# Last layer of a four-layer kernel: new due times for a batch's turned rows and folded keys

## What is computed

```python
var = jnp.mean(jnp.square(hidden_states), axis=-1, keepdims=True)
normed = hidden_states * jax.lax.rsqrt(var + EPS) * norm_w
q = split_heads(normed @ wq)              # 16 heads of 64
k = split_heads(key_value_states @ wk)    # 77 keys per batch
v = split_heads(key_value_states @ wv)
attn = softmax(einsum('bhqd,bhkd->bhqk', q, k))
ctx = einsum('bhqk,bhkd->bhqd', attn, v)
return hidden_states + ctx @ wo
```

## Time and profile before

| | |
|---|---|
| median of 3 runs | 2225.31 us (2221.91 to 2230.49) |
| time of the profiled execution | 2232.05 us |
| its span (first to last instruction) | 2230.3 us |
| mean granted clock of TensorE | 0.971 of 2.4 GHz |
| last layer in the profile | 1875.7 to 2230.3 us |
| borders in the last layer | about 1950, 2036 and 2122 us |

### The profile page before, as it was taken

The page is one execution under the profiler, slowest core; times in us unless marked ns, Lnnn a source line. Parts: engine busy times, 40 slices in busy tenths (PEclk is TensorE's granted clock), DMA queues, the critical chain, the costliest instruction groups (busy, mean ns, idle before and its releaser), DMA issues. The chain is left out here.

```text
span 2230.3 us, 38605 instructions
## 1 busy us (share of the span) xinstructions
PE 2013.3 (90%) x14610; PEld 1309.0 (59%) x14610; DVE 1386.9 (62%) x3054; ACT 1137.6 (51%) x1750; POOL 769.4 (34%) x1012
## 2 busy tenths in 40 slices
PE   4999999999998879998999899998989998999989
PEld 2333433343342258876566575765666667888989
DVE  4876776685767655645545554451677884866655
ACT  2265565555545666651645545363445553555444
POOL 3023124113212353311624526253111201756656
PEclk8799999999998999998999999999999999999999
DMA  6705403510730000018460716320422210000000
GB/s 146 140 7 113 60 1 68 89 23 36 113 76 1 1 15 1 1 55 122 92 108 21 143 17 131 66 66 1 162 86 86 85 58 1 11 10 13 16 13 20
DMA packets 77774, 126.68 MB, mean 57 GB/s; under 512 B 16650, under 2 KB 34826, under 8 KB 77582
## 3 DMA queue, kind: packets, MB, share of 16 engines
q1 hardware_dynamic: 74966, 122.63, 26.0%
q10 hardware_dynamic: 2624, 1.58, 0.2%
HBM read 93.59 MB, written 30.32 MB: 56 GB/s over the span
## 5 line engine op out<-in xcount | busy, mean ns | idle before, releaser
L1099 DVE TENSOR_REDUCE nmx_causal<-banks 128x1 f32<-128x333 f32 (+4 forms) x896 | 435.6, 538 | 174.1 <-PE banks L830 172.3
L988 ACT ACTIVATE probs_causal<-banks 128x1024 f32<-128x1024 f32 (+5 forms) x384 | 330.8, 899 | 258.3 <-PE banks L855 254.4
L830 PE MATMUL banks<-ks_causal,qs_causal 96*128 96x333 bf16 (+4 forms) x896 | 271.7, 339 | 13.8 <-DVE nmx_causal L1099 7.6
L753 POOL TENSOR_SCALAR_AFFINE_SELECT probs_window<-probs_window 128x512 f32<-128x512 f32 (+1 forms) x272 | 162.0, 602 | 258.0 <-ACT probs_window L988 247.0
L753 POOL TENSOR_SCALAR_AFFINE_SELECT probs_causal<-probs_causal 128x512 f32<-128x512 f32 (+2 forms) x160 | 92.4, 578 | 455.7 <-ACT probs_causal L988 455.4
L855 PE MATMUL banks<-qs_causal,ks_causal 97*128 97x512 bf16 (+5 forms) x896 | 209.6, 329 | 19.8 <-ACT probs_causal L988 16.0
L1099 DVE TENSOR_REDUCE nmx_window<-banks 128x2 f32<-128x384 f32 (+2 forms) x320 | 143.0, 460 | 104.5 <-PE banks L830 100.8
L879 PE MATMUL banks<-probs_causal,v_causal 128*17 128x512 f32 (+5 forms) x1792 | 185.8, 488 | 0.0
L988 ACT ACTIVATE probs_window<-banks 128x768 f32<-128x768 f32 (+2 forms) x128 | 99.7, 785 | 102.6 <-PE banks L855 102.1
L828 PEld LDWEIGHTS banks<-below,identb 128*128 128x128 bf16 x512 | 49.4, 98 | 173.5 <-DVE nmx_causal L1099 125.2
L830 PEld LDWEIGHTS banks<-ks_causal,qs_causal 96*128 96x128 bf16 x896 | 86.5, 99 | 103.5 <-DVE nmx_causal L1099 60.9
(11 more groups left out here) (261 smaller groups left out, 4099.9 us busy)
## 6 DMA issues: line engine op xcount, KB each, us to landing
fs_masked<-in_fside SPq DMA_DIRECT2D x32, 616.0 KB, 3.7
ks_causal<-zk SPq DMA_DIRECT2D x96, 137.6 KB
ks_window<-zk SPq DMA_DIRECT2D x96, 137.6 KB
qs_causal<-zq SPq DMA_DIRECT2D x96, 128.0 KB
qs_window<-zq SPq DMA_DIRECT2D x96, 128.0 KB
zk<-parts_causal SPq DMA_DIRECT2D x24, 275.2 KB, 2.9
zk<-parts_window SPq DMA_DIRECT2D x24, 275.2 KB, 2.4
zq<-parts_causal SPq DMA_DIRECT2D x24, 256.0 KB, 6.9
```

What stands on the lines that cost most here:

```text
L753: pool.affine_select(out=v, in_=v, compare_op=ALU.is_ge, fill=0.0, base=const, pattern=[[0, QH], [by_c, wd]], channel_multiplier=by_p).the ...
L830: ins = pe.matmul(bk[:, c:c + m], qs[q][0:KR, h, t * P:(t + 1) * P], ks[q][0:KR, h, key:key + m], start=cover is None, stop=True, skip_gro ...
L988: ins = act.activation(dst, src, ACT.Exp, scale=DH ** -0.5)
L1099: dve.tensor_reduce(dst, src, AX.X, ALU.max, negate=True).then_inc(emptied_v, 1)
```

## The change

Three due times of `folded_schedule` are changed. No instruction is added, removed or resized, and no semaphore or tile.

```diff
@@ folded_schedule @@
         if b:
             early = t0 - 8
             for half in range(2):
                 for k in range(ND):
-                    fill(t0 - 1.65 + (2 * half + k) / 10, ("turn", b, half, k), "sv")
+                    fill(t0 - 7.4 + 9 * half + k, ("turn", b, half, k), "sv")
         else:
             early = t0 - 4
             for half in range(2):
                 for k in range(ND):
-                    fill(early + (2 * half + k) / 10, ("turn", b, half, k), "sv")
+                    fill(early + 6 * half + k / 10, ("turn", b, half, k), "sv")
         pool += [(early, ("kbd", b)), (t0 + 0.2, ("vbd", b, 0)), (t0 + 0.2, ("vbd", b, 1))]
         for n, (pp, kk) in enumerate((pp, kk) for pp in range(4) for kk in range(ND)):
-            fill((t0 - 1.6 if b else t0 - 3) + n / 8, ("fold", b, kk, pp), "sv")
+            fill(t0 - 2.7 + n / 4 if b else t0 - 3 + n / 8, ("fold", b, kk, pp), "sv")
```

## The result

The changed kernel takes 2238.28 us (median of 12 runs, 2232.28 to 2248.55), the kernel before 2226.52 us (12 runs, 2220.52 to 2236.55). The ratio is 1.0054, 95% interval 1.0037 to 1.0071: slower by 0.54%, some 12 us (8 to 16).

The account below looks back on a forecast made before the run. PE was taken to bind except at borders and the layer's start, where the loop around two banks binds. Borders of +3.6, +1.75 and +1.75 us and -1.5 at the start gave +5.6: 2231 us, range 2216 to 2240.

Parts of the forecast that it names:

- A: First half's turns moved early, before the border: transposes wait for DVE to empty a bank; +3.45 us, +3.85 at batch 1.
- C: Second half's turns moved late, behind the border: transposes wait for DVE; +2.5 us, +3.4 at batch 1.
- B: Border stretch, tile 7's score to next batch's second score: shorter mostly because turns left; -4.2 us, -3.7 at batch 1.
- D: Start of the last layer: two turns leave the head, first score 1.8 us earlier, some lost on DVE; -1.5 us.
- signs of being wrong: No long waits at line 2286, border stretch above 20 us, or clock below 0.9 in the windows behind A.
- clock rival: Clock falls to 1.2 GHz behind A, 2.3 us each, three times: +12.5 us, 2238 us; chance 0.10.
- B brings nothing: At borders, DVE's shift and invert within the folds cost as much as the turns did: 2243 us; chance 0.09.
- A and C hidden: Transposes behind the moved turns need not wait, 0.8 us each: -8.8 us, 2216.5 us; chance 0.15.
- the whole border saved: All waits at the three borders go, 7.6 us each: 25.2 us faster, 2200 us; chance 0.08.

Follow-up runs that it names:

- run 1: Kernel before with only the first half's two turns per batch moved early, ahead of the border; ratio to the kernel before 1.0025, 2242.34 us beside 2233.99.
- run 2: Kernel before with only the second half's two turns per batch moved late, behind the border; ratio to the kernel before 0.9995.
- run 5: Changed kernel with each batch's four turns each directly behind a tile's last transposes, in front of 21 matmuls; ratio to the kernel before 0.9965.
- run 6: Changed kernel with 24 unread identity transposes filling PE's wait behind the first half's second turn; ratio to the kernel before 1.0040.
- run 7: run 5's kernel with the eight folds of a batch spread over the border; ratio to the kernel before 0.9876, 2202.20 us.
- run 3: Kernel before with only the folds' due times changed; ratio to the kernel before 0.9993.
- run 4: Kernel before with only the layer's start changed, two turns of batch 0 behind scores 0 1 0; one profiled execution, 2238.78 us.
- run 8: run 7's kernel with out part 0 of tile 5 in front of tile 6's transposes, except in the last batch; ratio to the kernel before 0.9883, 2204.65 us.

## Why the prediction was right in kind and too small

It said +5.6 us and no measurable change, 2216 to 2240; it came out at +12 us (8 to 16), inside the range, at its slow end. By its own line of 0.5% the measured 0.54% is just on the slower side, to which it gave 0.21; the interval, 0.37 to 0.71, lies on both sides of that line.

**A** held to 0.03 us where the clock was full: 3.42 at batch 3 for 3.45, 3.85 at batch 1 for 3.85. **C** held: 2.57 for 2.5, 3.50 for 3.4. That a transposition two places behind a turn waits for DVE's shift and invert is shown by putting the wait in by itself (runs 1 and 2) and by taking it away: in run 5 the waits at line 2286 for a turn are gone, and A at batch 3 takes 3.05 us less, at full clock in both traces.

**B** was forecast at -4.2 and read -3.4 at batches 2 and 3; run 5 has -4.3 at full clock. So there the walk was right and the clock took 0.8 to 0.9. At batch 1 the forecast was -3.7 and -2.6 was read, at a clock of 0.83 (1958.18:1977.72 above). There the walk had a term that was too large: it put 1.0 us for norm36 and close36 among the folds (and its 18.4 is 18.26 by its own terms), but at a like clock batch 1's B is longer than batch 3's by only 0.15 us in run 5 and 0.5 in run 6, and in run 7, at full clock, all three are equal. So the clock took more than 1.1 at that border, and the two misses partly cancelled. Its reading, that the leaving turns and not the folds' pace shorten the border, is shown by runs 1 to 3.

**D** was -1.87 for -1.5. The first score came 1.88 us earlier, as said, and nothing of it was lost on the way to scores 0 3 0, where the walk had put 0.3 for DVE. The first fold waits 1.3 us for POOL's keys, as said. In run 4 it was -3.6 at a higher clock, so what the start gives hangs on that too.

**The step that failed** is the clock. The sum gave it no price; it stood only among the rivals, as three falls behind A, 6.9 us, with a chance of 0.10. In the profiled execution it was one fall behind A (0.46 inside A and 0.98 behind it at batch 2) and a part of every border (what B misses of its forecast: 1.1, 0.9 and 0.8). These 4.2 us, less 0.4 at the start, are the distance from 5.6 to the 9.5 that the trace shows. The estimate of 2.3 us per fall was high: 1.4 was the one seen, and 1.6 and 1.5 the two in run 1. One of the prediction's own signs of being wrong was met: the clock behind A was to stay at 0.9 or above, and it was 0.66 in the five us behind the wait of batch 2. That the clock rival's sum, 12.5 us and 2238, is the measured number to 0.5 us is luck: it has three falls behind A at 2.3 us and none at the borders, and the trace has one fall there and all three borders.

The Trainium skill, "TensorE: Matmul & The Clock Gate", section on HAM oscillation, says that waits between bursts of matmuls bring the array back to half rate. It was right about the direction, and only in part: at A three of six bare waits had a fall behind them, and the same border list ran at 0.80 and at 1.00 in run 4.

Of the rival that B brings nothing, and of those with A and C hidden or the whole border saved, nothing is left for this change. The last one came true in another kernel: run 8 takes 10.3 us out of a border's stretch and puts 1.9, 0.4 and 1.1 in elsewhere, 6.9 net against the 7.6 that the prediction called the most.

Between the 9.5 us of the trace and the 12 of the runs, 2.5 are not accounted for. They lie inside the interval; how often the clock falls in other executions was not profiled. So the ring's share is shown, and the clock's share of the 12 us is read from one trace of each kernel and stays open for the others.

## What to carry to other kernels

Where a ring has two banks, a token's price is not its own time but when the *next but one* user is due: place it behind the last short use and in front of the longest stretch of work that doesn't use the ring, and look at what stands ahead of it on the engine that empties it. Moving a burst out of a crowded place is worth nothing if it lands directly in front of another user of the same banks. Walk each new place by hand, from start to start; here that gave A and C to within 0.1 us at full clock.

## What the runs showed of the hardware that was not expected

How closely this kernel's spread from execution to execution goes with the clock of TensorE. Over 51 executions of the kernel before, made beside these experiments, the time goes from 2220.58 us at a mean granted clock of 0.978 to 2246.14 at 0.963, with a correlation of -0.93 and 1.8 us for each 0.001. The changed kernel's 12 executions have a mean of 2239.2 us at 0.9682; the line through the 51 gives 2235.9 there, so an estimated 3.3 us would remain at equal clock, against 5.6 in the walk. That compares sets of runs that were not made together, and run 6, with the same ring waits, lies 5.9 us above the line; so it bears out a loss of a few us beside the clock and not its size.

The same border code took 23.12 us at a granted clock of 1.00 and 25.83 at 0.80 within one execution (run 4), PE being busy 17.9 of the 23.12. With PE busy 12.7 of 12.87 the clock was full at every border (run 8). Over all traces: where folds stand in a row or among turns (the two kernels and runs 1 to 6), the clock was below full in 18 of 24 B stretches; where the folds are spread (runs 7 and 8), in none of 6. So closing gaps paid twice.
